# Layer 0 of a four-layer graph network: ScalarE's norm sums split in two, ELU's minimum on GpSimd, ELU behind the eighth weight

## The reference: what is computed

```python
h = jnp.maximum(_layernorm(x, axis=-1), 0.0)        # eps 1e-5
Wh = jnp.einsum('bni,io->bno', h, W)
s1 = Wh @ a1;  s2 = Wh @ a2
e = leaky_relu(s1[:, :, None] + s2[:, None, :], 0.2) + mask
attention = softmax(e, axis=2)
x = x + elu(einsum('bnm,bmo->bno', attention, Wh))
```

## Time and profile before

| what | value |
|---|---|
| median of 3 runs | 2041.74 us (2040.82 to 2042.96) |
| the profiled execution's own time | 2039.39 us |
| its span in the profile | 2037.6 us |
| TensorE busy in the span | 1908.2 us (94%) |
| VectorE busy | 1685.1 us (83%) |
| ScalarE busy | 1245.3 us (61%) |
| GpSimd busy | 1037.3 us (51%) |
| granted TensorE clock, mean | 0.986 of full speed |

### The profile page before, as it was taken

One profiled execution on the slowest core, in us unless ns is written; L12 is line 12 of the kernel. 1 busy time (PEld: TensorE's weight loads), 2 busy tenths in 40 slices (PEclk: granted clock), 3 DMA queues, 4 the chain that ended last, 5 costly groups with the idle time before them and its releaser, 6 DMA issues.

```text
span 2037.6 us, 94849 instructions
## 1 busy us (share of the span) xinstructions
PE 1908.2 (94%) x43528; PEld 1566.7 (77%) x43528; DVE 1685.1 (83%) x2005; ACT 1245.3 (61%) x1860; POOL 1037.3 (51%) x738
## 2 busy tenths in 40 slices
PE   5888779999999999999999999999999999989998
PEld 4777679987777777777777777777777777767787
DVE  5888878868778888888888888888888888867998
ACT  4877545426666666666666666666666666644342
POOL 6566678723235445454454554545545445354653
PEclk8999889999999999999999999999999999999999
DMA  6000000001111111111111111111111111101111
GB/s 178 4 4 3 3 2 3 2 12 34 34 34 34 34 34 30 37 31 33 35 30 37 31 33 35 30 36 32 34 34 34 34 34 34 34 13 24 24 25 34
DMA packets 88254, 61.22 MB, mean 30 GB/s; under 512 B 45616, under 2 KB 86832, under 8 KB 87856
## 3 DMA queue, kind: packets, MB, share of 16 engines
q1 hardware_dynamic: 85632, 54.57, 10.9%
q10 hardware_dynamic: 2224, 0.59, 0.1%
HBM read 8.98 MB, written 4.19 MB: 6 GB/s over the span
## 4 chain that ended last, share of the span: by engine, by line
PE 67%; DVE 13%; ACT 7%; POOL 7%; issue 2%; DMA 1%; SPq 1%; POOLq 0%; ACTq 0%; DVEq 0%
PE ACC L1547 29%; PE S L1727 23%; PE S L1706 5%; DVE ring L1326 4%; PE AX L1770 3%; DVE ring L1194 2%; PE AX L1779 2%; PE AX L1747 2%; POOL sp_log L759 1%; POOL ln_sq L762 1%; ACT st_x L871 1%; ACT ring L1000 1%; PE AX L1527 1%; DVE ch_rden L1311 1%; ACT st_x L867 1%
## 5 line engine op out<-in xcount | busy, mean ns | idle before, releaser
L1547 PEld LDWEIGHTS ACC<-V,ring 128*64 128x64 f32 x28672 | 961.9, 139 | 202.4 <-DVE ring L1194 52.2
L1326 DVE TENSOR_TENSOR ring<-ring,mask_self_t 128x1024 f32<-128x1024 f32 x640 | 892.5, 1404 | 194.3 <-ACT ring L1000 189.8
L1547 PE MATMUL ACC<-V,ring 128*64 128x65 f32 x28672 | 981.2, 224 | 51.3 <-DVE ring L1194 32.5
L1000 ACT ACTIVATE ring<-S,dot_bias 128x1024 f32<-128x1024 f32 x640 | 713.3, 1115 | 409.5 <-PE S L1727 372.9
L1727 PE MATMUL S<-FA 128*64 128x512 f16 x5120 | 666.0, 382 | 1.8 <-DMA FA<-lo 1.5
L1727 PEld LDWEIGHTS S<-FA 128*64 128x64 f16 x5120 | 253.6, 110 | 161.5 <-ACT ring L1000 15.8
L1194 DVE SCALAR_TENSOR_TENSOR ring<-S,pair_q,mask_t 128x1024 f32<-128x1024 f32 x256 | 314.7, 1273 | 20.9 <-ACT S L914 5.0
L775 POOL TENSOR_TENSOR EV_both<-score,recip 128x512 f32<-128x512 f32 x64 | 124.3, 1942 | 315.5 <-DVE score L1335 315.4
L1706 PE MATMUL S<-parts,mask_t 128*128 128x128 bf16 x3072 | 176.1, 220 | 14.0 <-DVE X L1315 13.8
L1706 PEld LDWEIGHTS S<-parts,mask_t 128*128 128x128 bf16 x3072 | 174.3, 99 | 15.6 <-issue 15.5
L768 POOL TENSOR_TENSOR V<-v_pairs,bh_bc 128x512 f32<-128x512 f32 x64 | 96.5, 1507 | 118.2 <-ACT v_pairs L1020 118.2
(11 more groups left out here) (126 smaller groups left out, 1993.2 us busy)
## 6 DMA issues: line engine op xcount, KB each, us to landing
FA<-hi SPq DMA_DIRECT2D x320, 64.0 KB, 2.1
FA<-lo SPq DMA_DIRECT2D x320, 64.0 KB, 2.0
X<-in_x SPq DMA_DIRECT2D x16, 256.0 KB, 4.9
ring<-in_adj SPq DMA_DIRECT2D x8, 512.0 KB, 8.0
out_x<-X SPq DMA_DIRECT2D x16, 256.0 KB, 2.6
wh<-in_wh_t ACTq DMA_DIRECT2D x2, 64.0 KB, 6.4
bh_bc<-in_bh ACTq DMA_DIRECT2D x1, 128.0 KB, 9.3
w_gat<-in_w_gat ACTq DMA_DIRECT2D x4, 16.0 KB, 4.0
```

Of the source, the lines that this page charges most:

```text
L1000: act.activation(ring[:, jt, :], S[jt % 2][:, :], ACT.Exp, bias=dot_bias[:, n % 2:n % 2 + 1])\
L1326: dve.tensor_tensor(ring[:, jt, :], ring[:, jt, :], mask_self_t[:, jt, :], ALU.mult)\
L1547: last = pe.matmul(acc_of(t)[rows, :], ring[:, jt, t * P + c * CUT:t * P + (c + 1) * CUT], values, start=(jt == 0 and t % 4 == 0), stop=(j ...
```

## The change

It has three parts, all in layer 0.

1. `late_norm_sums` is cut in two. `late_shifts`, the eight accumulated means, goes ahead of `gat_factors`, that is between the copy that makes `h_t` and the copy of V. `late_squares`, the eight squares and the two small steps, stays last.
2. ELU's minimum moves from ScalarE to GpSimd. A new `tensor_scalar` with `min` against 0 stands right behind the division and reads its result; ScalarE's exponential loses its scale of -1, and its Relu step is gone.
3. VectorE's `gat_elu` stands behind the eighth weight of the unit and no longer behind the seventh.

```diff
@@ gat_divide, GpSimd
                 pool.tensor_tensor(tiles(o[:, :]), accs[:, :, 1:D + 1], cols(recip[:, :]), ALU.mult).then_inc(gat_o, 1)
+                if layer == 0:
+                    wait(pool, elu_made, b)
+                    pool.wait_ge(gat_o, n + 1)
+                    pool.tensor_scalar(below[:, :], o[:, :], 0.0, None, ALU.min).then_inc(elu_below, 1)
@@ ScalarE
-            def late_norm_sums(b):
+            def late_shifts(b):
...
                 for t in range(T):
                     act.activation(st_x[:, 0, t * D:(t + 1) * D], x_of(b)[:, t, :], ACT.Copy, scale=-1.0 / (8 * D),
                                    accum_out=st_shift[:, par, t:t + 1]).then_inc(late_shifted, 1)
+
+            def late_squares(b):
...
             def gat_below(b):
-                act.wait_ge(gat_o, b + 1)
-                act.activation(below[:, :], o[:, :], ACT.Relu, scale=-1.0).then_inc(elu_below, 1)
                 act.wait_ge(elu_below, b + 1)
-                act.activation(below[:, :], below[:, :], ACT.Exp, scale=-1.0).then_inc(elu_exp, 1)
+                act.activation(below[:, :], below[:, :], ACT.Exp).then_inc(elu_exp, 1)
@@ gat_layer, ScalarE
                         h_relu(layer, cur + 2)
+                    if late_stats(layer, cur) is not None:
+                        late_shifts(late_stats(layer, cur))
                     if cur + 1 < B:
                         gat_factors(layer, cur + 1)
...
                     if late_stats(layer, cur) is not None:
-                        late_norm_sums(late_stats(layer, cur))
+                        late_squares(late_stats(layer, cur))
@@ gat_layer, VectorE
-                        if jt == 6 and cur > 0 and layer == 0:
+                        if jt == 7 and cur > 0 and layer == 0:
                             gat_elu(cur - 1)
```

More of the change, by code:

```diff
@@ L868, in late_norm_sums @@
                                    accum_out=st_shift[:, par, t:t + 1]).then_inc(late_shifted, 1)
+            def late_squares(b):
+                par, n = b % 2, b - EARLY
                 act.wait_ge(late_shifted, T * (n + 1))
```

## The result

The changed kernel took 2035.52 us (median of 9 runs, 2033.06 to 2038.96), the kernel before 2042.59 us (9 runs) beside it. The ratio is 0.9964, with a 95% interval of 0.9955 to 0.9972: about 7 us faster. The forecast was 20 us, and 2035.5 lies above its range. The direction held, the size did not.

The account below looks back on a forecast made before the run. The prediction took layer 0 to be bound by a 13.89 us ring of ScalarE and GpSimd, falling to 11.95. Gains of 16.8 us by unit 10 and 20.4 by unit 13 gave 2041.74 - 20.4 = 2021.3 us, range 2017.5 to 2030.

Parts of the forecast that it names:

- The ring of ScalarE and GpSimd: Layer 0's chain of waits between these engines, repeating every 13.89 us; forecast to fall to 11.95 us.
- Means: Eight means on ScalarE, 2.01 us, would be hidden behind h_t with 1.2 us to spare before the biases.
- The 0.67 us at the start: In unit 1 the means would make L902, the start of the factor V, 0.67 us late, once.
- the price m: Length of GpSimd's new minimum on 512 elements, taken as 0.6 us, with 0.45 as lower end.
- The upper bound: Upper end for the minimum's length: GpSimd's two-input addition to X, 1.24 us, since the minimum has one input.
- 2.68 + m: Start of ScalarE's exponential after L902 with the minimum on GpSimd; whole round 11.35 + m us.
- Units 14 and 15: Minimum ahead of layer 1's steps loses 0.8 us in unit 15, ELU's move offsets; taken as zero, 1 us either way.
- nine intervals that all lose 1.94 us: From unit 1 to unit 10, 9 x 1.94 - 0.67 = 16.8 us gained at the start of V's factor.
- The two-input price: Rival, 0.14: GpSimd's minimum costs as much as a two-input operation, 1.24 us; round 12.59 us, time 2028.7 us.
- VectorE as bound: Rival, 0.13: GpSimd still holds up ELU, VectorE's load stays 12.08 us; 14.5 us gained, 2027.2 us.
- The slow minimum: Rival, 0.07: GpSimd's minimum is slow, and the kernel loses from 2.54 us; 3 us gives 2052 us.
- Units 11 to 13: VectorE's f copy in unit 11 comes 12.89 us after unit 10's L902; two 11.4 us loads reach unit 13, 20.4 us gained.

Follow-up runs that it names:

- e1_means: Kernel before with only the eight means moved up, between the copy for h_t and the copy of V: 2029.38 against 2044.54 us, ratio 0.9926.
- e5_prices: Kernel before with nine GpSimd operations on scratch tiles added behind its last step: minimum on 512 elements 1.48 us, two-input operation 1.26, multiply-then-add 0.62.
- e4_means_elu8: Kernel before with means moved up and ELU behind the eighth weight, Relu kept on ScalarE: 2021.38 against 2044.54 us, ratio 0.9891.
- e2_elu8: Kernel before with only ELU moved behind the eighth weight: 2042.50 against 2044.54 us, ratio 0.9995.
- e7_end_relu: Changed kernel with ScalarE's Relu and no GpSimd minimum in the last three ELUs: 2031.42 against 2043.09 us for the kernel before, ratio 0.9946.
- e11_cheap_stand_in: Changed kernel with GpSimd's minimum replaced by multiplying by 1 and adding 0: 2024.79 against 2042.88 us for the kernel before, ratio 0.9909.

## Why the prediction was wrong

**What bounds the kernel: right.** The ring of ScalarE and GpSimd set the pace, and VectorE was the next bound: `e1_means` met it at 11.99 us with ELU in its old place (the forecast's load with a contended ELU was 12.08).

**Means: right.** Hidden behind `h_t`, with L908 still waiting 1.39 us for the biases (forecast 1.2). The 0.67 us at the start showed too: L908 of unit 1 comes 11.61 us after that of unit 0 (51.70 and 40.09), where it was 11.00 us before (51.80 and 40.80), so it is 0.61 us late.

**The step that failed: the price m.** I took 0.6 us from two rows that had neither the operation nor the shape: the biases, multiply-then-add on one element, and the cast, 128 elements to bfloat16. Scaling them up did no harm, since multiply-then-add and a copy take 0.62 and 0.61 us on 512 elements (`e5_prices`). The operation did: a single minimum takes 1.49. The upper bound failed too. I took the two-input addition, 1.24 us, as the end "since the minimum has one input", and no row said that fewer inputs cost less. With m = 1.49 the ring is 12.84, the gain at unit 10 is 9 x 1.05 - 0.67 = 8.8 us (measured 8.6, counted from unit 0). The Trainium skill (GPSIMD Engine Reference, section 4.1) calls one-input work on GpSimd roughly line-rate, and has 769 ns for 512 elements in a tight loop in its section 3.1. The copy's 0.61 us is under that, the minimum's 1.48 us nearly twice as much: here the measurement decides.

**A comparison that was missing.** The rows held what Relu cost the ring. The exponential starts 3.19 us behind L902 with Relu, and 2.68 + m with the minimum. So part 2 gains only for m below 0.51 us, under the value that I took. Parts 1 and 3 alone (11.85 us, `e4_means_elu8`) would have beaten the forecast's own 11.95. I priced the sum of the parts and never each part against leaving it out.

**Units 14 and 15: wrong in size.** I had zero, give or take 1 us; they gave back 3.5. ELU behind the eighth weight did bring the end forward, by 1.5 us: in `e2_elu8` the stretch from the last `f` copy to the third block of matmuls is 73.71 us and not 75.22. The minimum costs 4.6 us there (`e7_end_relu`). The changed kernel's chain of waits runs through three of them, one in each unit and one behind unit 15:

```profile
215.22 1.48 POOL below L619
...
232.96 1.49 POOL below L619
...
256.56 1.50 POOL below L619
```

Together they are 4.47 us. I had called the first hidden, priced the second, and left the third out. With m = 0.62 the stretch is still 76.43 us, 1.2 over before.

**Units 1 to 3: wrong by 1.6 us.** In `e11_cheap_stand_in` the start of unit 10 came 15.0 us early, 15.2 counted from unit 0, not 16.8. I counted nine intervals that all lose 1.94 us. The one from unit 2 to 3 still took 77.24 - 64.15 = 13.09 us and lost 0.8, and L908 waits there for the copy of V, not for the biases. VectorE has five small steps more in unit 2 and no wait there but the short gaps behind `f_max`: it was the bound, not the ring. The five took 2.3 us (from 61.61), against 1.2 before (from 61.84): one of them, a two-input step on 2 elements (L1153), took 1.27 us and not 0.16, and it now fell beside GpSimd's addition to X (61.93, 1.27 us).

**The rivals.** The two-input price (0.14) was the right mechanism with a price still too low: m = 1.24 against 1.49. VectorE as bound (0.13) is what `e1_means` shows, not the changed kernel. The slow minimum (0.07) gave the reason that held, that an operation's kind can dominate its price, with m = 3 far too high. ELU took 0.86 us in its new place (the median of its sixteen), inside the forecast's 1.0.

**Units 11 to 13, and the clock.** With m = 1.49 and L908 of unit 10 at 166.76, my steps put the `f` copy of unit 11 at 166.76 + 12.89 + 0.89 = 180.5 us and unit 13's at 203.3. They came at 182.09 and 204.89. Ahead of the first, TensorE's sums at 175.15 took 1.78 us in place of 1.15, in a stretch with a granted clock of 0.66 of full speed, and the `f` copy of unit 11 waited 1.95 us for TensorE. `e7_end_relu` has the same order up to unit 13, and in its execution the granted clock is 1.00 from 165 to 205 us. There L912, its L908, starts unit 10 at 167.62, and the `f` copy of unit 11 comes at 181.39 with a wait of 0.40 us, where the same steps put it (181.4). Unit 13's comes at 204.49, 0.3 us behind them. From unit 10's `f` copy to unit 13's it is 37.20 us with the fall and 35.95 without, so the fall cost about 1.3 us. This compares two executions. No edit takes the fall away.

## What to carry to other kernels

Price a new operation by a row of the same operation, not by a row with fewer inputs or a near shape. Where no row has it, no row gives a bound either: the slowest row of this shape in the ring, 1.27 us, was still under the minimum's 1.49. A look at nine scratch operations behind the kernel's end settles it. Write the ring's period as a formula in the unknown price, solve it for the break-even against leaving that edit out, and give each part of a change its own price. In a ring of two engines, moving work into waits that are already there paid: 15 us for the means, 23 with ELU behind the eighth weight, 27 with the mask copy too. Handing a step to the other engine of the same ring cost 15 us by itself. Before comparing times of two traces, take off what the two executions differed by at a step ahead of the change.

## What the runs showed of the hardware

GpSimd's `tensor_scalar` on 128x512 float32 showed three prices by its operations: 0.62 us for multiply-then-add, 1.48 to 1.50 us for a single minimum, maximum, multiplication or addition, 1.92 to 1.94 us for the other pairs tried. The single minimum grows by 2.5 ns per element from 256 to 512 elements (0.84 to 1.48 us). Multiplying and adding together cost less than half of multiplying alone (0.62 and 1.49 us). The price list ran each form once, in a single execution; the minimum (1.48 to 1.49), min-add (1.92 to 1.93) and multiply-then-add (0.62 to 0.63) were the same in all sixteen units. Why the pairs differ so, no run shows.

The granted clock of TensorE falls for short stretches in layer 0, at places that move with the schedule. Stretches of 5 us (busy us and count of PE, PEld, DVE, ACT, POOL; then the granted clock, 1.00 being 2.4 GHz), and the `f` copy of unit 11, of after:

```profile
125.00:130.00 5.00, 5.00 (x117) 3.39 (x116) 3.74 (x5) 3.69 (x17) 4.13 (x7) 0.73 0.01 3
...
175.00:180.00 5.00, 4.85 (x96) 3.51 (x98) 5.00 (x6) 4.16 (x22) 3.47 (x5) 0.66 0.01 3
...
182.09 0.17 DVE L1212 COPY f<-AX 128x8 f32<-128x8 f32 x1 [1.95 <-PE AX L1577]
```

and of before:

```profile
140.00:145.00 5.00, 3.48 (x62) 2.94 (x64) 4.57 (x5) 4.20 (x22) 1.67 (x2) 0.73 0.01 3
```

Between 100 and 190 us these are two falls in after and one in before, the one of before reaching past 145. A stretch with 0.66 or 0.73 holds both of the clock's levels, 2.4 and 1.2 GHz. In the 5 us ahead of them TensorE was busy for 3.07 and 3.22 us in after (the clock of the first of these is 0.92, so that fall had begun), and 4.07 us in before. The intervals of the ring stayed at 12.85 and 13.89 us through the falls near 127 and 143 us, so a fall cost nothing while ScalarE and GpSimd set the pace. In unit 11, where VectorE and TensorE do, it seems to have cost 1.3 us, by the comparison with `e7_end_relu`. The clock is lowered for longest in units 14 and 15: stretches of 5 us have 0.50 to 0.84 from 220 to 255 us in after and from 230 to 265 us in before. No run prices that one.
